# GpSimd instead of VectorE adds the gated attention into x

## The reference

```python
mod = silu(c) @ ada_w + ada_b
shift_msa, scale_msa, gate_msa, shift_mlp, scale_mlp, gate_mlp = jnp.split(mod, 6, axis=-1)
x = x + gate_msa[:, None, :] * attention(modulate(norm(x), shift_msa, scale_msa))   # 16 heads of 9
x = x + gate_mlp[:, None, :] * (gelu(modulate(norm(x), shift_mlp, scale_mlp) @ fc1 + b1) @ fc2 + b2)
```

## Time and profile before

| | |
|---|---|
| three runs, median | 1398.58 us (1395.71 to 1400.19) |
| profiled execution, its own time | 1397.83 us |
| its span in the profile | 1396.1 us |
| mean granted TensorE clock | 0.977 |
| VectorE, `add_attention` (L1191) | x64, 35.3 us busy, mean 552 ns |
| GpSimd, `add_mlp` (L629) | x64, 53.8 us busy, mean 841 ns |
| VectorE, maxima (L1124) | x512, 329.0 us busy, mean 684 ns |

### The profile page before, as it was taken

One profiled execution on the slowest core, in us unless ns is written; L12 is line 12 of the kernel. 1 busy time (PEld: TensorE's weight loads), 2 busy tenths in 40 slices (PEclk: granted clock), 3 DMA queues, 4 the chain that ended last, 5 costly groups with the idle time before them and its releaser, 6 DMA issues.

```text
span 1396.1 us, 36486 instructions
## 1 busy us (share of the span) xinstructions
PE 1221.2 (87%) x13058; PEld 772.4 (55%) x13058; DVE 1067.1 (76%) x2812; ACT 881.6 (63%) x2123; POOL 260.5 (19%) x382
## 2 busy tenths in 40 slices
PE   6366778999969999999999999999989999998887
PEld 4212345555546666666666666666655665666654
DVE  3845678888878888888888888888878888886642
ACT  0032456668747777777777777777777676776563
POOL 2001111211222222222222222222212222221011
PEclk9999899999989999999999999999999999999998
DMA  6404442434544444444444444444478667776410
GB/s 180 122 0 112 113 119 83 102 96 122 130 114 123 125 126 127 128 125 129 127 127 126 126 127 130 130 130 131 126 147 151 142 141 135 124 126 138 77 27 26
DMA packets 209362, 163.63 MB, mean 117 GB/s; under 512 B 82825, under 2 KB 187217, under 8 KB 209185
## 3 DMA queue, kind: packets, MB, share of 16 engines
q1 hardware_dynamic: 200800, 153.61, 46.2%
q10 hardware_dynamic: 8384, 7.69, 1.9%
HBM read 98.05 MB, written 62.41 MB: 115 GB/s over the span
## 4 chain that ended last, share of the span: by engine, by line
PE 49%; DVE 23%; issue 10%; ACT 7%; DMA 4%; ACTq 3%; SPq 3%; DVEq 0%; POOL 0%; POOLq 0%
PE lin L1523 10%; PE lin L1539 7%; DVE maxima L1124 7%; PE o_bank L1476 6%; PE score_bank L1369 5%; PE score_bank L1413 3%; PE st_bank L1444 3%; ACT h2T L726 2%; PE lin L1527 2%; DVE stats L986 2%; ACT p_room L740 2%; DVE gated L1182 2%; PE lin L1509 2%; PE score_bank L1385 2%; ACT hT_last L721 2%
## 5 line engine op out<-in xcount | busy, mean ns | idle before, releaser
L1124 DVE TENSOR_REDUCE maxima<-score_bank 128x4 f32<-128x512 f32 x512 | 329.0, 684 | 69.0 <-PE score_bank L1413 66.3
L740 ACT ACTIVATE p_room<-st_bank 128x512 f32<-128x512 f32 x512 | 276.7, 596 | 107.4 <-PE st_bank L1444 70.4
L638 POOL TENSOR_TENSOR part_low<-qk_rest,part_mid 96x512 bf16<-96x512 f32 x96 | 113.8, 1186 | 389.7 <-DVE part_mid L1107 389.7
L1539 PE MATMUL lin<-w_f,gelu 128*128 128x144 f32 (+1 forms) x1280 | 173.2, 291 | 0.8 <-DVE gated L1182 0.8
L1523 PE MATMUL lin<-h2T,w_h 128*128 128x512 f32 (+1 forms) x320 | 169.5, 628 | 4.1 <-ACT h2T L726 2.3
L1476 PE MATMUL o_bank<-p_room,v_room 128*32 128x128 f32 x4096 | 167.7, 282 | 0.0
L1539 PEld LDWEIGHTS lin<-w_f,gelu 128*128 128x128 f32 (+1 forms) x1280 | 163.9, 193 | 2.5 <-DVE gated L1182 1.2
L1413 PE MATMUL score_bank<-stack_room 62*128 62x128 bf16 x2048 | 103.9, 222 | 53.3 <-DVE qk_rest L1102 19.1
L846 ACT ACTIVATE gelu<-lin 128x512 f32<-128x512 f32 (+1 forms) x160 | 90.9, 589 | 81.3 <-PE lin L1527 80.8
L1413 PEld LDWEIGHTS score_bank<-stack_room 62*128 62x128 bf16 x2048 | 59.9, 95 | 127.7 <-issue 49.5
L629 POOL TENSOR_TENSOR x<-x,gated 128x288 f32<-128x288 f32 x64 | 53.8, 841 | 408.2 <-DVE gated L1182 408.2
(11 more groups left out here) (193 smaller groups left out, 2192.8 us busy)
## 6 DMA issues: line engine op xcount, KB each, us to landing
stack_room<-stack_dram SPq DMA_DIRECT2D x192, 256.0 KB, 5.9
stack_dram<-part_high SPq DMA_DIRECT2D x64, 288.0 KB, 3.5
gates<-gates_dram SPq DMA_DIRECT2D x64, 288.0 KB, 3.4
norm_room<-stack_dram SPq DMA_DIRECT2D x64, 256.0 KB, 6.0
stack_dram<-part_mid SPq DMA_DIRECT2D x64, 192.0 KB, 2.6
stack_dram<-part_high SPq DMA_DIRECT2D x64, 144.0 KB, 3.3
stack_dram<-part_mid SPq DMA_DIRECT2D x64, 96.0 KB, 2.8
stack_dram<-part_low SPq DMA_DIRECT2D x64, 96.0 KB, 2.1
```

The source lines that it names most:

```text
L638: eng.tensor_tensor(part_low[:, T, :], qk_rest[:, T, :], part_mid[:, T, :], ALU.subtract)\
L740: eng.activation(probs[:, i % PBUFS, :], st_bank[i % 2][:, :], ACT.Exp, scale=float(HD) ** -0.5)\
L1124: eng.tensor_reduce(maxima[:, b, CH * c:CH * c + CH], bank_of(f"S{i}")[:, :].rearrange("p (h k) -> p h k", h=CH), AX_X, ALU.max)\
L1539: ins = eng.matmul(o, gelu[0:k, T, b * TOK:(b + 1) * TOK], w_f2[l][0:k, T, :], start=T == 0, stop=T == FCT - 1)
```

## The change

`add_attention(g, h)` goes from VectorE's program to GpSimd's, with the same operands and the same semaphore. It gets one more `need`, for n1_ready of its group, since VectorE's `normalise(g, 0)` reads the same rows of x and was ahead of the addition on VectorE's own queue before. On VectorE it stood behind `residual(P, 1, 0)` in the middle of the body and behind `divide(g, 2)` near its end. On GpSimd it stands ahead of `add_mlp(Q, 0)` and at the very end of the body.

```diff
@@ GpSimd @@
+            def add_attention(g, h):
+
+                if not ok(g):
+                    return
+                need(eng, "proj_gated", g, h)
+                need(eng, "n1_ready", g, GB - 1)
+                eng.tensor_tensor(pair_of(g, h), pair_of(g, h), gated[0][:, h, :], ALU.add).then_inc(S["x_attn"], 1)
+
...
                 rstd_of(M, 0)
+                add_attention(P, 1)
                 add_mlp(Q, 0)
                 rstd_of(P, 1)
                 add_mlp(Q, 1)
...
                 if not normed_heads(M):
                     low(M, 0)
+                add_attention(g, 0)
@@ VectorE @@
-            def add_attention(g, h):
-
-                if not ok(g):
-                    return
-                need(eng, "proj_gated", g, h)
-                eng.tensor_tensor(pair_of(g, h), pair_of(g, h), gated[0][:, h, :], ALU.add).then_inc(S["x_attn"], 1)
...
                 residual(P, 1, 0)
-                add_attention(P, 1)
                 maxima_of(J, 0)
...
                 divide(g, 2)
-                add_attention(g, 0)
                 maxima_of(J, 4)
```

## The result

The changed kernel took **1382.23 us** in the median of four runs (1378.27 to 1389.28), the kernel before on the same chip 1397.45 us. The ratio is 0.9895 with a 95% interval of 0.985 to 0.994: 15.2 us less. The prediction was 1384.0 us, with 1377 to 1393 as its range, and faster at 0.88. The profiled execution is the slowest of the four, 1389.28 us (span 1387.5 us). Later runs of the same kernel (experiment 4) gave 1380.67 us and a trace of 1379.34 us. The two traces agree in what a body does and differ in the start and in single bodies, so I read bodies from the first and whole stretches from the second.

What follows compares the result with a forecast made beforehand. No engine is full; gains exist only where TensorE waits for VectorE behind an addition. 9.8 (layers 1 and 2 plus token bodies) + 2.2 (token bodies) + 2.0 (layer 0) = 14.0 us; 1397.8 - 14.0 = 1384 us, range 1377 to 1393.

Steps and rivals of the forecast that it cites:

- rival 2: TensorE's earlier queries only lengthen its wait for ScalarE's h2T; 9.8 us lost, 1393.6 us; chance 14%.
- h0, layers 1 and 2: add_attention(g, 0), near the body's end: moving it ends TensorE's queries' wait for maxima, 0.42 us, 17 times, 7.1 us.
- the whole wait goes: Near the body's end, the first maximum ends 0.69 us earlier, more than TensorE's 0.42 us wait, with 0.27 us spare.
- h0, token bodies: add_attention(g, 0), in bodies ordering tokens for layer 3: moving it ends the queries' six waits for maxima, 2.7 us.
- h1, layers 1 and 2: add_attention(P, 1), near the body's middle: time won on VectorE becomes a wait for scores; between 0 and 0.37 each, taken as 0.
- h1, token bodies: add_attention(P, 1), mid-body where tokens are ordered for layer 3: maxima of pair 1 start 0.36 us earlier, six bodies, 2.2 us.
- Layer 0: Bodies of layer 0: 0.31 us for the second half's addition, 0.37 for the first's, three bodies each, 2.0 us.
- GpSimd's additions at nothing: The 64 additions put on GpSimd, 0.79 us each, 51 us more busy time, delay nothing and cost 0.
- the interference: GpSimd's moved additions slowing VectorE's maxima beside them in both places; taken as 0, bounded by 0.62 us each.
- 1: Mid-body second-half additions in layers 1 and 2 pay too, 16 x 0.37 = 5.9 us more, 1378 us; chance 9%.
- 3: Slower: GpSimd's late first-half addition, behind part_low, holds VectorE up, 0.62 us each, 1403.6 us; chance 3%.
- 4: Slower: the sum in x comes late and is waited for, 64 additions 0.335 us longer, 1419 us; chance 2%.

Runs made afterwards that it cites:

- experiment 1: Against the kernel before, only the addition of each group's first half moved to GpSimd, the second half's staying on VectorE: 1388.07 us, ratio 0.9938.
- experiment 2: Against the kernel before, only the addition of each group's second half moved to GpSimd, the first half's staying on VectorE: 1395.02 us, ratio 0.9994.
- experiment 8: The kernel before run again without an edit, one execution for a second trace: 1395.95 us.
- experiment 3: Kernel before, all additions kept on VectorE, the first half's moved from ahead of the maxima of pair 4 to behind them: 1386.06 us, ratio 0.9932.
- experiment 5: Changed kernel, with GpSimd's attention addition taking only 4 of 288 columns: 1378.82 us, ratio 0.9869.
- experiment 12: Changed kernel, with the first half's addition back on VectorE behind the maxima of pair 4, the second half's on GpSimd: 1383.15 us, ratio 0.9888.
- experiment 6: Changed kernel, with two of four bn_stats of the second norm put ahead of the maxima of pair 1 in layers 1 and 2: 1384.3 us, ratio 0.9894.
- experiment 7: Changed kernel, with the second norm's statistics put behind the maxima of pair 2 in layers 1 and 2: 1392.33 us, ratio 0.9955.

## Why the prediction was right, and where not

The total was 1.8 us off, and that closeness is partly luck: the largest term was 4.0 us too small, the others 1.2 us too large between them, and the runs before were 0.4 us faster than the one that the sum started from. The path that the prediction named, TensorE's queries waiting for maxima behind h0, was the right one. The range was said to reach to rival 2, whose 1393.6 us lies just outside it.

- **h0, layers 1 and 2: the mechanism right, the term too small.** The step "the whole wait goes" held, but 0.42 us each was the wrong size. The body is 0.65 us shorter, so the 17 waits are worth 11.1 us and not 7.1. The earlier trace rows had the number: 730.20 - 729.50 is 0.70 us from start to start, and flips without a wait start 0.11 us apart in the trace after.
- **h0, token bodies: wrong as a sure gain.** I took the six waits of the earlier trace rows, 2.7 us, for a gain. With h0 alone the wait goes too, but five bodies are only 0.11 us shorter in the mean. For layers 1 and 2 I had followed what comes after the wait; here I hadn't, and VectorE's waits for DMA in these bodies (14.3 us from 1050 to 1240 us, before) were in no part of the sum. What TensorE gains at the queries it waits again for the maxima behind order(J, 0), held by the transfer of the next stack, in three of the four bodies of experiment 1 in the table above; the fourth is 0.43 us shorter.
- **h1, layers 1 and 2: right.** It turned into a wait of 0.50 us for scores, and nothing was gained (experiment 2). It was 16 x 0.37 us that could have been counted wrongly, and the end of the scores, 715.11 against a start at 715.14, told it. The wait that some 0.4 us were expected for is 0.50.
- **h1, token bodies: right**, 0.36 predicted and 0.35 measured with h1 alone. Together h0 and h1 give 0.63 us and not the 0.8 of the prediction: the additions in a row of token bodies of experiment 4 are 37.62 us apart in the mean ((1246.26 - 1133.40) / 3), against 38.25 before ((1226.01 - 1111.27) / 3). Six bodies make 3.8 us, where the two terms had 2.7 + 2.2 = 4.9.
- **Layer 0: the sum right, its parts not.** A body there lasts 41.68 us in the trace of experiment 8 (334.23 to 375.91, the additions of h1) and 41.30 us in that of experiment 4 (331.22 to 372.52), so 0.38 us less; at most five bodies make 1.9 us, where 2.0 stood. With h0 alone the like bodies take 41.57 us, with h1 alone 41.40: 0.1 us for h0, where I had 0.37, and 0.27 for h1, where I had 0.31, but counted over up to five bodies and not three. In experiment 3 they take 41.68, so in layer 0 moving h0 behind the maxima gives nothing. Single bodies of the layer vary by over 1 us in every kernel, so no total can confirm any of this.
- **GpSimd's additions at nothing: right**, by experiment 5, to within what its total can tell. The maxima beside them keep 1.28 and 1.29 us, so the interference that I bounded by 0.62 us each didn't come.
- **Sum as measured in bodies:** 11.1 + 3.8 + 1.9 = 16.8 us, where the prediction had 14.0, against 15.2 in the first comparison and 15.6 in experiment 4 (1396.27 - 1380.67), both with intervals of 2 to 6 us on either side.
- **Rivals.** 1 fell with experiment 2. 2 fell: the wait for h2T is 6.6 us as before, and the queries' 0.65 us come out at the body's end. ScalarE does move with the queries. 3 and 4 fell with experiment 5, and with the 4.8 us by which the sum in x is early.

The rule of the Trainium skill (GPSIMD Engine Reference, section 4.1 Engine selection) gives elementwise additions to VectorE and has GpSimd about twice as slow with two inputs. The traces have 1.7 times (794 ns against 459), and yet the kernel with the slower engine is the faster one. Experiment 12 fits the rule all the same: h0 is as well off on VectorE, once it stands behind the maxima.

## What to carry to other kernels

Before moving an operation to another engine, try it one place later on its own: where something is waited for right behind it, that place can be the whole gain, as it was in layers 1 and 2. Price a TensorE stall by the distance between the starts on its two sides, less the distance that unstalled neighbours show, not by the idle time printed. And when a wait goes, look who is next. In experiment 6 a wait of 0.5 us was replaced by one of the same length for ScalarE; in experiment 7 the waits that came were longer than the one that went; in the token bodies a transfer that had held up VectorE alone before took most of the gain back.

## What the runs showed of the hardware

- A TensorE stall shown as 0.42 us cost 0.59 us from start to start (0.70 against 0.11) and 0.05 us in the matmuls behind it (1.07 us against 1.02).
- Start and single bodies of one and the same kernel differ by several us: the start lasts 205 to 213 us over the fourteen traces, and one token body of the changed kernel took 41.1 us in one trace and 37.3 us in the next. An effect of a few us is seen in the length of a repeated body, not in one trace's span.
- VectorE's maxima of a 128x512 bank in PSUM took 1.28 us a pair with GpSimd's addition beside them and without; VectorE's additions and max_parts, which read SBUF, took up to 0.77 us for 0.46 and 0.79 us for 0.18 beside GpSimd.
- The mean granted clock of TensorE doesn't order these times: the kernel before took 1397.83 us at 0.977 and 1395.95 us at 0.956.
